# Per-round weight sums, two result banks in turn, and two reorderings in a four-layer graph kernel

## The reference, cut to what matters

```python
# layer 0: attention of each node over its hyperedges
coefs1 = softmax(where(H > 0, se[:, None, :], NEG), axis=-1)        # (b, n, e)
g = einsum('bne,benf->bnf', coefs1, elu(beta * h + (1 - beta) * agg))  # sum over edges of a node
...
x = layernorm(x + layer0(x))
# layer 2: three powers of the adjacency, node-specific weights from an embedding (D = 16)
x_g = einsum('knm,bmc->bnkc', A_stack, x)
out = einsum('bnki,nkio->bno', x_g, einsum('nd,dkio->nkio', embedding, weight)) + bias
x = layernorm(x + out)
```

## Time and profile before

| what | us |
|---|---|
| runs of the kernel | 732.07 median of 3 (731.03 to 732.12) |
| the profiled execution | 729.97, its span 728.2 |
| layer 0's rounds (start of tile 0's zeroing to end of tile 7's sums) | 103 to 196 |
| layer 2's products | 490 to 645 |
| PE busy / DVE / ACT / POOL over the span | 665.5 / 421.7 / 337.2 / 289.7 |

### The profile page before, as it was taken

How to read it: one execution, slowest core, us unless ns; L and a number is a source line. 1 busy time by engine, 2 the same in 40 slices (tenths; PEclk the granted TensorE clock), 3 DMA queues, 4 the chain that set the end, 5 groups by cost and what they waited for, 6 DMA issues and landing times.

```text
span 728.2 us, 9826 instructions
## 1 busy us (share of the span) xinstructions
PE 665.5 (91%) x3420; PEld 460.7 (63%) x3428; DVE 421.7 (58%) x970; ACT 337.2 (46%) x645; POOL 289.7 (40%) x267
## 2 busy tenths in 40 slices
PE   6898988878799889999999999999999989899993
PEld 2796766656566767533333358887776767678883
DVE  1676656777439942466877856114565757561166
ACT  1861234544367442356566544413446565355214
POOL 0270105565526810001424257024667676760045
PEclk9999999999989799999999999999999999999998
DMA  9120030000000036000100000000000000000013
GB/s 329 34 87 2 1 116 1 1 0 1 2 1 1 4 79 153 1 0 1 59 0 1 1 1 1 1 0 1 2 1 1 0 1 1 1 1 2 1 28 88
DMA packets 14995, 18.34 MB, mean 25 GB/s; under 512 B 10128, under 2 KB 10128, under 8 KB 14944
## 3 DMA queue, kind: packets, MB, share of 16 engines
q1 hardware_dynamic: 14432, 16.06, 7.7%
q10 hardware_dynamic: 512, 1.60, 0.6%
HBM read 11.37 MB, written 2.10 MB: 18 GB/s over the span
## 4 chain that ended last, share of the span: by engine, by line
PE 53%; DVE 7%; POOL 7%; ACT 3%; issue 2%; ACTq 0%; POOLq 0%; DVEq 0%
PE PS L1503 8%; PE PS L1390 7%; PE PS L1373 7%; PE PS L1516 5%; PE PS L1556 4%; PE PS L1545 4%; POOL LN_Y L163 3%; DVE arena L2139 2%; PE PS L182 2%; PE PS L1482 2%; PE PS L1489 2%; PE PS L189 2%; PE PS L1566 2%; DVE LN_ST L140 2%; PE PS L1252 1%
## 5 line engine op out<-in xcount | busy, mean ns | idle before, releaser
L2139 DVE SCALAR_TENSOR_TENSOR arena<-PS,WT,arena 128x256 f32<-128x256 f32 x160 | 77.4, 484 | 59.2 <-PE PS L1516 34.6
L1713 ACT ACTIVATE arena<-PS,spare 128x1024 f32<-128x1024 f32 x64 | 70.8, 1109 | 49.8 <-DVE spare L2076 49.6
L1503 PE MATMUL PS<-WH,KK 128*128 128x512 f32 x256 | 87.2, 404 | 6.1 <-POOL KK L1917 5.6
L2076 DVE TENSOR_REDUCE spare<-PS 128x1 f32<-128x1024 f32 x64 | 75.6, 1219 | 23.8 <-PE PS L1373 23.7
L163 POOL TENSOR_TENSOR LN_Y<-LN_V,CN 128x16 f32<-128x16 f32 (+1 forms) x18 | 49.4, 2745 | 73.7 <-DVE LN_V L155 73.7
L1781 ACT ACTIVATE spare<-PS,WT 128x256 f32<-128x256 f32 x96 | 38.8, 472 | 68.5 <-DVE arena L2139 66.7
L1873 POOL TENSOR_TENSOR arena<-arena,spare 128x128 f32<-128x128 f32 x32 | 13.9, 433 | 134.7 <-DVE spare L2082 124.0
L1390 PE MATMUL PS<-arena 128*64 128x512 f32 x256 | 62.0, 605 | 1.5 <-POOL arena L1873 1.4
L1503 PEld LDWEIGHTS PS<-WH,KK 128*128 128x128 f32 x256 | 48.0, 188 | 24.0 <-issue 12.4
L1503 PE MATMUL PS<-WL,KK 128*128 128x512 f32 x128 | 50.1, 391 | 0.0
L1373 PE MATMUL PS<-arena 64*128 64x512 f32 x192 | 48.2, 618 | 1.4 <-ACT arena L1713 1.4
(11 more groups left out here) (293 smaller groups left out, 1491.8 us busy)
## 6 DMA issues: line engine op xcount, KB each, us to landing
arena<-in_adj_tr SPq DMA_DIRECT2D x8, 512.0 KB, 5.8
arena<-in_x_tr SPq DMA_DIRECT2D x4, 512.0 KB, 7.9
arena<-in_x_nat SPq DMA_DIRECT2D x1, 2048.0 KB, 9.2
arena<-arena SPq DMA_DIRECT2D x7, 256.0 KB, 2.8
arena<-arena SPq DMA_DIRECT2D x12, 128.0 KB, 2.3
spare<-in_w SPq DMA_DIRECT2D x2, 512.0 KB, 4.1
out<-arena SPq DMA_DIRECT2D x4, 256.0 KB, 3.0
out<-arena SPq DMA_DIRECT2D x8, 128.0 KB, 2.2
```

What stands on the lines that cost most here:

```text
L1503: ins = pe.matmul(acc, x[:, t % 2, b, :], w[:, k, c], start=(first and n == 0), stop=(not first and n == 2), skip_group_check=True)
L1713: act.activation(EF[2 * (i % RING) + par], banks("S", 2 * i + par).rearrange("p a c -> p (a c)"), ACT.Exp, bias=NMX[:, i, par:par + 1], ac ...
L2076: dve.tensor_reduce(NMX[:, i, par:par + 1], banks("S", 2 * i + par), AX.XY, ALU.max, negate=True).then_inc(max_ready, 1)
L2139: dve.scalar_tensor_tensor(acc, PS[:, four_banks(t, j), d * F:(d + 1) * F], WT[:, e:e + 1], acc, ALU.mult, ALU.add).then_inc(acc_step, 1)
```

## The change

In layer 0's rounds:
- Tile sums go to bank 4 for even tiles and bank 7 for odd ones (`sums_bank`). TensorE zeroes a bank after `acc_out` of the tile but one before, no longer of the tile before.
- The weights' sums are no longer kept in PSUM over a tile's rounds. Each round starts them anew in eight columns of bank 5; ACT copies them, inside the loop and behind a new wait for the end of the round, to ZR (`zr_out`); POOL adds ZR to ZS inside its loop, behind a new wait for that (`zs_added`); DVE's reciprocal waits for `zs_added`. TensorE waits for `zr_out` ahead of `edge_rows`, which writes to the same bank.
- TensorE's gather C_ stands ahead of `edge_rows`; DVE's shift of chunk A_ stands ahead of `from_first`.

In layer 2: POOL's `low_parts(t + 1)` stands ahead of `scales(i)`.

```diff
+        def sums_bank(t):
+            return 4 + 3 * (t % 2)
@@ POOL, in the round
+                        pool.wait_ge(zr_out, j + 2)
+                        pool.tensor_tensor(ZS[:, t, :], ZS[:, t, :], ZR[:, :], ALU.add).then_inc(zs_added, 1)
                     if t + 2 < NT:
                         low(t + 2)
@@ ACT, end of the round
                         likely()
+                        act.wait_ge(acc_done, j + 2)
+                        act.activation(ZR[:, :], PS[:, 5, ZN_AT:ZN_AT + B], ACT.Copy).then_inc(zr_out, 1)
                     if t + 2 < NT:
                         high(t + 2)
-                    act.wait_ge(acc_done, first[t + 1] + 1)
-                    act.activation(GN[:, t, :], PS[:, 4, :], ACT.Copy)
-                    act.activation(ZS[:, t, :], PS[:, 7, ZN_AT:ZN_AT + B], ACT.Copy).then_inc(acc_out, 1)
+                    act.activation(GN[:, t, :], PS[:, sums_bank(t), :], ACT.Copy).then_inc(acc_out, 1)
@@ DVE
                         mix(A_, 2)
+                        shift(A_, 2)
                         dve.wait_ge(selg_ready, j + 1)
                         dve.wait_ge(nt_ready, j + 1)
                         from_first(at).then_inc(ns_half, 1)
-                        shift(A_, 2)
@@ PE
-                    if t >= 1:
-                        pe.wait_ge(acc_out, t)
-                    pe.matmul(PS[:, 4, :], zero16[:, 0:P], zero16[:, :], start=True, stop=False, skip_group_check=True)
-                    pe.matmul(PS[:, 7, ZN_AT:ZN_AT + B], zero16[:, 0:P], zero16[:, 0:B], start=True, stop=False, skip_group_check=True)
+                    if t >= 2:
+                        pe.wait_ge(acc_out, t - 1)
+                    pe.matmul(PS[:, sums_bank(t), :], zero16[:, 0:P], zero16[:, :], start=True, stop=False, skip_group_check=True)
                     pe.wait_ge(hpl_ready, min(t + 2, NT))
                     with pe.Fori(first[t], first[t + 1]) as j:
+                        pe.wait_ge(z_ready, CHUNKS * j + 1)
+                        gather(t, C_)
+                        pe.wait_ge(zr_out, j + 1)
                         pe.wait_ge(ns_ready, j + 2)
                         edge_rows(t_next)
-                        pe.wait_ge(z_ready, CHUNKS * j + 1)
-                        gather(t, C_)
@@ layer 2, POOL
                     add_scaled(t, 0)
+                    if t + 1 < NT:
+                        low_parts(t + 1)
                     for i, (first, n) in enumerate(NORMS):
                         if first + n == t:
                             scales(i)
                     if t + 1 < NT:
-                        low_parts(t + 1)
                         init(t + 1)
```

More of the change, by code:

```diff
@@ L291, in program @@
         iota = CN[:, C_IOTA:C_IOTA + ROUND].rearrange("p (c n) -> p c n", n=P)
-        SMALL_AT, ZN_AT = CHUNKS * E, 0
+        SMALL_AT, ZN_AT = CHUNKS * E, 3 * P
+        ZR = sb("ZR", [P, B])
+        zr_out, zs_added = sem("zr_out"), sem("zs_added")
+        def sums_bank(t):
+            return 4 + 3 * (t % 2)
         A_, B_, C_ = range(CHUNKS)
@@ L353, in _ @@
                 pool.memset(zero16[:, :], 0.0).then_inc(zero_set, 1)
+                pool.memset(ZS[:, :, :], 0.0)
                 pool.wait_ge(sl, 1)
@@ L512, in _ @@
                 first = first_rounds(act)
+                act.activation(ZR[:, :], zero16[:, 0:B], ACT.Copy).then_inc(zr_out, 1)
                 industry_out(3)
@@ L767, in _ @@
                     if t >= 1:
-                        dve.wait_ge(acc_out, t)
+                        dve.wait_ge(zs_added, first[t])
                         dve.reciprocal(ZS[:, t - 1, :], ZS[:, t - 1, :]).then_inc(rn_ready, 1)
                 dve.wait_ge(acc_out, NT)
+                dve.wait_ge(zs_added, first[NT])
                 dve.reciprocal(ZS[:, NT - 1, :], ZS[:, NT - 1, :]).then_inc(rn_ready, 1)
@@ L987, in scatter @@
                             pe.wait_ge(w_ready, CHUNKS * j + (c + 1))
-                            return pe.matmul(PS[:, 4, :], NST[:, c, :], S1[:, c, :], start=False, stop=True, skip_group_check=True)
+                            return pe.matmul(PS[:, sums_bank(t), :], NST[:, c, :], S1[:, c, :], start=False, stop=True, skip_group_check=True)
+                        pe.wait_ge(z_ready, CHUNKS * j + 1)
+                        gather(t, C_)
+                        pe.wait_ge(zr_out, j + 1)
                         pe.wait_ge(ns_ready, j + 2)
                         edge_rows(t_next)
-                        pe.wait_ge(z_ready, CHUNKS * j + 1)
-                        gather(t, C_)
                         pe.wait_ge(nst_out, j + 1)
@@ L1009, in _ @@
                         for c in range(CHUNKS):
-                            ins = pe.matmul(PS[:, 7, ZN_AT:ZN_AT + B], NST[:, c, :], CC[:, c, :], start=False, stop=True,
-                                            skip_group_check=True)
+                            ins = pe.matmul(PS[:, 5, ZN_AT:ZN_AT + B], NST[:, c, :], CC[:, c, :], start=(c == 0),
+                                            stop=(c == CHUNKS - 1), skip_group_check=True)
                         ins.then_inc(acc_done, 1)
```

## The result

The changed kernel takes 764.8 us (median of 4 runs, 764.66 to 764.99) against 732.1 us (731.03 to 732.12): a ratio of 1.045, 95% interval 1.043 to 1.047. That is slower, as forecast, but by 32.7 us where 10.1 were forecast, and outside the range (735.5 to 750). The profiled execution's span is 762.9 us, 34.7 above the 728.2 of before.

What follows compares the result with a forecast made beforehand. Layer 0's rounds were taken as set by the time from round end T to scatter A plus 6.87 us. 10.1 + 3.2 - 0.6 + 1.3 - 3.9 = +10.1 on 732.07 gave 742.2 us; range 735.5 to 750.

Steps and rivals of the forecast that it cites:

- PE's chain: Layer 0's rounds, from round end T: ZR copy, high, low, gather C, edge rows, edges, turn_edges at T + 5.5; 12.7 us a round.
- POOL's chain: Layer 0's rounds, from T: low, multiplication, add, CC, weighting, scatter A at T + 6.2; 13.1 us; both chains together +10.1.
- TensorE's clock: Layer 0: new waits drop the clock to its low level in four of six rounds, 0.8 us each: +3.2, between 0 and 9.
- the 12.5 us round: Layer 0, profile before: round with mean granted clock 0.86, read as a low stretch costing 1.3 us.
- The first rival: Layer 0: clock stays low in nearly all rounds, or the port costs its full price: +15.9, 748 us; chance 0.17.
- Shared port: Layer 0: POOL's low, multiplication and add beside DVE's bend of chunk A: 0 in the sum, upper end +2.5.
- Ends of the stage: Layer 0's start and end: round 0 starting earlier, -0.6, and POOL finishing later before the barrier, +1.3.
- Round 0: Layer 0's first round: gather C starts some 1.3 us earlier and breaks up the 2.49 us wait: -0.6, between 0 and -1.3.
- The end: Behind tile 7 in layer 0: POOL adds, multiplies tile 6 and adds until T + 2.95; the barrier waits: +1.3.
- Layer 2: POOL's low part ahead of the power removes PE's waits for it: -3.9, between -5.6 and -2.
- The third wait: Layer 2, tile 6: PE's longest wait for POOL's low part, 2.0 us, gives only 0.35 because POOL's combine doesn't move.

Runs made afterwards that it cites:

- the fill: Changed kernel with matmuls of zeros in both TensorE pauses of a round (nine at the head, five behind edge rows, two behind turn_edges): 737.8 us, ratio 1.007.
- with the head filled: Changed kernel with only nine matmuls of zeros ahead of TensorE's wait for POOL's low part at the round's head: 753.2 us, ratio 1.026.
- the run with `high` behind the copies: Kernel before with one line moved: ACT's high part of tile t + 2 behind the two copies of the sums: 757.4 us, ratio 1.033.
- with gather C back: Changed kernel with TensorE's gather of chunk C behind edge rows again, as before the change: 743.8 us, ratio 1.016.
- the runs with one pause filled: Changed kernel with zero matmuls only at the round's head (753.2 us), or only behind edge rows and turn_edges (747.6 us).

## Why the prediction was off, point by point

**PE's chain and POOL's chain: right.** The steps came within 0.15 us: gather C at T + 2.4 (forecast 2.5), turn_edges at T + 5.35 (5.5), scatter A at T + 6.25 (6.2). With the clock kept up the gaps sum to +12.3, forecast +10.1. Of the 2.2 between them 0.45 is the first gap (13.15, not 12.7), and this is the fill itself: turn_edges started at T + 5.5 as forecast, and the two zero matmuls behind it held scatter A up by 0.43. The five middle rounds took 13.2 to 13.4, not 13.1: 0.86. The last took 12.36, not 11.5: POOL's add took 1.62 us there and the weighting of chunk A 1.40, longer beside DVE than the rows I took (1.26 and 1.04).

**TensorE's clock: the step that failed.** It was put at +3.2 with an upper bound of 9. It measured 27.9 us (28.3 without the fill's 0.43). The mechanism was named, but the number of low rounds was guessed low: I took four of six, and all seven gaps had one, even the last, which has no wait for a low part. The price per round was far off: I took 0.8 and at most 1.5, from the 1.3 of the 12.5 us round, and it was 27.9 / 7 = 4.0. I wrote that the clock came back within a round each time, but had not read how long it was away. In the 12.5 us round the low stretch was about 3.4 us long, and PE was busy in all of it: at half speed that can't cost more than 1.7. In the changed kernel it lasted 10.2 us and covered scatter A and the small sums, where PE is the bound: 10.97 us for what took 6.87. Nothing in the trace of before bounded its length. The bound should have been the whole second half at half speed, up to 6.87 us a round, 48 us for seven, and not the one case seen. The first rival was the right one in kind and had the same wrong price; 748 is still 17 us short. The range failed with this one term: the upper end had 9 us for it.

**Shared port: 0 was a little low.** In the middle rounds the add took 1.53 instead of 1.26, the multiplication 1.04 as before; in the last gap the add took 1.62.

**Ends of the stage.** Round 0 gave 1.6 us (forecast 0.6, bound 1.3): gather C, at 103.79, broke up the wait, and the clock stayed at 1.00. In the kernel before it hadn't: the mean was 0.87 from 103 to 116.2, a third low round that the prediction didn't see. Nor does the code of round 0 keep the clock up by itself: with the head filled, which leaves round 0 as it is, the first T came 5.4 us later. The end cost 1.7 (forecast 1.3): the add took 1.52 beside DVE's multiplication.

**Layer 2: right mechanism, size off.** -5.5 us against -3.9. The third wait went too, which I had left at 0.35; it reached my bound of -5.6.

In the span: -1.6 + 12.3 + 27.9 + 1.7 - 5.5 = 34.8, against 34.7 measured. With the forecast's clock term the rest gives +10.1 to within 0.1; that is luck, since the errors of the other terms cancel. The median stands 2.1 above the profiled execution before, and 0.05 under it after, so the medians differ by 32.7.

**What stays open.** Why the low level lasts 3.4 us in one round and 10.2 or more in another. In the run with `high` behind the copies PE worked 12.1 us without a pause at the low level before it rose; with gather C back it rose after 1 us of unbroken work. Idle time ahead of it does not order these cases. Nor is it known why the clock falls in one round and not in the next with the same pauses, as with the head filled. None of this touches the size of the clock's share, which the run with both pauses filled gives. The Trainium skill, "TensorE: Matmul & The Clock Gate", section "A second HAM failure mode: psum-queue depth-cycling", tells of short idle times between groups of matmuls that make the clock swing between its two levels; the runs with one pause filled agree with that much, and no run here shows what ends a low stretch.

## What to carry to other kernels

A wait that is put ahead of TensorE's work costs its own length and, where the clock falls, up to the whole length of the busy stretch behind it once more; bound the cost by that stretch at half speed, not by the one low stretch that the trace shows. Here two short pauses close together were worse than either alone (764.8 us against 753.2 and 747.6), and moving a ready gather back into the hole between two dependent steps gave 21 us; it did not keep the clock up in every round. A few zero matmuls tell quickly whether time is lost to the clock, and may cure it. Before a step is put into a loop with a wait, list what stands behind that wait in the same queue: here `high` and `low`, which had been free.

## What the runs showed of the hardware

- With the head filled, PE's pauses in a round were 0.2 to 0.4, 1.19 and mostly 0.37 us. The granted clock fell to its low level in three of six such rounds, and not in the other three.
- A low stretch can outlast 12.1 us of unbroken matmuls (36 records, in the run with `high` behind the copies); another, with gather C back, ended after 1 us of them.
- Zero-valued bf16 matmuls hold the clock at 1.00: 48 of them in layer 0's rounds made a kernel 19 us faster (740.2 to 721.5, the first with a wide spread), 110 made the changed kernel 27 us faster.
- `to_last` on DVE took 1.40 us where GpSimd's add had started ahead of it, and 0.62 where it started first; then GpSimd's instruction was the longer one (its 128x8 add 0.59 beside `to_last`, 0.20 alone).
